# Attention's weighing in 32 bits, the experts' second bias on VectorE, and a combination with four neighbouring tokens per partition

## What is computed

```python
q, k, v = (qkv[0] * scale, qkv[1], qkv[2])        # 16 heads of 8 channels
# logits over the 7 x 7 neighbours of a pixel, plus a relative bias
attn = softmax(logits, -1)
out = sum_t attn[..., t, None] * v_at_neighbour_t
x = x + (out @ proj_w.T + proj_b)
probs = softmax(layernorm(x) @ W_router); topk_p, topk_i = top_k(probs, 2)
for e in range(8):
    h = relu(x_flat @ W1[e] + b1[e])               # 128 -> 512
    y = h @ W2[e] + b2[e]                          # 512 -> 128
    out = out + combine[:, e:e + 1] * y
```

## Time and profile before

| | |
|---|---|
| median of 3 runs | 3155.05 us (3146.11 to 3156.77) |
| the profiled execution | 3149.2 us, its span 3147.4 us |
| mean granted TensorE clock | 0.904 |
| busy: PE, DVE, ACT, POOL | 79%, 75%, 67%, 75% of the span |
| attention | from the start to about 2300 us |
| experts | about 2366 to 2963 us |
| combination | about 2963 us to the end |

### The profile page before, as it was taken

The page is one execution under the profiler, slowest core; times in us unless marked ns, Lnnn a source line. Parts: engine busy times, 40 slices in busy tenths (PEclk is TensorE's granted clock), DMA queues, the critical chain, the costliest instruction groups (busy, mean ns, idle before and its releaser), DMA issues. The chain is left out here.

```text
span 3147.4 us, 119476 instructions
## 1 busy us (share of the span) xinstructions
PE 2482.8 (79%) x34587; PEld 2108.7 (67%) x34692; DVE 2353.8 (75%) x12579; ACT 2122.5 (67%) x5724; POOL 2360.1 (75%) x2808
## 2 busy tenths in 40 slices
PE   4788887888788878888888878888709999999633
PEld 2677777777777777777777777777606666666522
DVE  2688887888788878888788878888746666666444
ACT  0677777777677777777777777777726777777400
POOL 2578888888888888888888888888946777777600
PEclk9999999999899999999999989999959999999855
DMA  2566555555555655555565555556455444444499
GB/s 49 145 126 119 121 124 119 114 122 118 112 106 122 123 118 110 118 117 117 114 120 118 118 109 119 121 117 123 92 99 94 93 92 93 93 93 92 98 314 299
DMA packets 743654, 378.47 MB, mean 120 GB/s; under 512 B 414595, under 2 KB 712227, under 8 KB 743078
## 3 DMA queue, kind: packets, MB, share of 16 engines
q1 hardware_dynamic: 690278, 235.46, 39.5%
q10 hardware_dynamic: 24192, 81.67, 9.9%
q0 software_dynamic: 28608, 54.48, 5.7%
HBM read 232.92 MB, written 98.11 MB: 105 GB/s over the span
## 5 line engine op out<-in xcount | busy, mean ns | idle before, releaser
L1004 ACT ACTIVATE pr<-sc,nmx 128x100 f32<-128x100 f32 x3136 | 922.3, 369 | 103.8 <-DVE nmx L670 100.6
L905 POOL TENSOR_TENSOR pl<-pt 100x512 f16<-100x512 f32 x784 | 815.3, 1040 | 217.9 <-ACT pt L1012 217.4
L670 DVE CUSTOM_DVE_ANT_0 sc<-bank,near 128x100 f32<-128x100 f32 x3136 | 632.3, 256 | 182.7 <-PE bank L490 133.4
L1012 ACT ACTIVATE pt<-bank 100x512 f32<-100x512 f32 x784 | 462.5, 590 | 365.9 <-PE bank L516 353.0
L490 PE MATMUL bank<-kimg,qexp 128*128 (+2 forms) x9408 | 651.5, 221 | 55.3 <-issue 40.0
L490 PEld LDWEIGHTS bank<-kimg,qexp 128*128 128x128 bf16 (+1 forms) x9408 | 567.7, 102 | 103.1 <-issue 71.7
L1385 POOL DMA_INDIRECT yrows<-ye,meta x420 | 451.1, 1074 | 188.6 <-issue 127.6
L516 PE MATMUL bank<-vwin,pt 100*128 100x65 bf16 (+1 forms) x6272 | 417.0, 199 | 202.7 <-DVE om L700 142.6
L516 PEld LDWEIGHTS bank<-vwin,pt 100*128 100x128 bf16 x6272 | 371.9, 102 | 277.1 <-issue 184.6
L911 POOL TENSOR_TENSOR oml<-om 128x256 f16<-128x256 f32 x784 | 483.4, 617 | 57.3 <-DVE om L700 35.4
L499 PE MATMUL bank<-cst_sb,pr 128*100 128x128 f32 x3136 | 503.9, 286 | 0.0
(11 more groups left out here) (150 smaller groups left out, 4665.4 us busy)
## 6 DMA issues: line engine op xcount, KB each, us to landing
vwin<-v_pix SPq DMA_DIRECT2D x1120, 60.5 KB
near<-bias_rows ACTq DMA_DIRECT2D x112, 600.0 KB
y<-yrows SPq DMA_DIRECT2D x112, 224.0 KB, 4.8
qexp<-qring SPq DMA_DIRECT2D x896, 14.0 KB
v_pix<-vrow SPq DMA_DIRECT2D x56, 225.8 KB
xin<-in_x SPq DMA_DIRECT2D x56, 224.0 KB
xres<-in_x SPq DMA_DIRECT2D x112, 112.0 KB, 4.6
x<-xres SPq DMA_DIRECT2D x112, 112.0 KB
```

The lines of the kernel that those rows point to most:

```text
L670: i = v.tensor_tensor_reduce(out=sc[:, ring(m, par), k, :], in0=ps_s[m % 2][:, k, :], in1=near[:, st, ct, k, :], scale=-1.0, scalar=-MASKE ...
L905: g.tensor_tensor(pl[:, m % 2], pt[:, m % 2], pt_h[:, m % 2], ALU.subtract).then_inc(s["t_out"], 1)
L1004: i = a.activation(pr[:, r, k, :], sc[:, r, k, :], ACT.Exp, bias=nmx[:, r, k:k + 1], scale=-1.0)
L1012: i = a.activation(pt[:, m % 2].rearrange("p a q -> p (a q)"), ps_t[m % 2][0:NKEY, :], ACT.Copy)
```

## The change

Three edits. In attention, `v_pix`, `vrow` and `vwin` hold 32-bit numbers (129 a pixel); `weigh` multiplies `pt` and `vwin` as they are, one 32-bit product for each block; `split_t`, `a_v_l` and the buffer `pl` are gone, and every station behind the transposes stands one step earlier. In the experts, the product for the second bias is gone and DVE adds the bias in PSUM, from a table `b2b` with all experts' biases on every partition, before it multiplies. In the combination, a partition holds four neighbouring tokens, so its rows of `y` are 2048 bytes in one piece, and DVE's last sum reorders the columns; the first four loads of x1 are issued before SP waits for the last scatters.

```diff
-L_T, L_V, L_P, L_H, L_F = 3, 5, 6, 7, 8
+L_T, L_V, L_P, L_H, L_F = 3, 4, 5, 6, 7
-        v_pix = nc.dram_tensor("v_pix", (B * IMG, 2, VW), BF16, kind="Internal").ap()
+        v_pix = nc.dram_tensor("v_pix", (B * IMG, VW), FP32, kind="Internal").ap()
-        vwin = asb("vwin", [NKEY, 2, NTILE, 2, VW], BF16)
+        vwin = asb("vwin", [NKEY, 2, NTILE, VW])
-        vrow = asb("vrow", [HALF, NROW, 2, VW], BF16)
+        vrow = asb("vrow", [HALF, NROW, VW])
-        pl = asb("pl", [NKEY, 2, 4, 128], FP16)
...
                 def weigh(J, m, par):
-                    pe.wait_ge(s["t_out"], n + 1)
+                    pe.wait_ge(s["th_done"], n + 1)
...
-                            p_h, p_l = pt_h[:, m % 2, 2 * t + blk, :], pl[:, m % 2, 2 * t + blk, :]
-                            v_h, v_l = (vwin[:, st, 2 * u + t, part, 64 * blk:64 * blk + 65].bitcast(dt)
-                                        for part, dt in enumerate((BF16, FP16)))
-                            for n, (a_, b_) in enumerate(((p_h, v_h), (p_h, v_l), (p_l, v_h))):
-                                mm = pe.matmul(ps_av[m % 2][:, 2 * t + blk, :], a_, b_, start=n == 0, stop=n == 2)
+                            mm = pe.matmul(ps_av[m % 2][:, 2 * t + blk, :], pt[:, m % 2, 2 * t + blk, :],
+                                           vwin[:, st, 2 * u + t, 64 * blk:64 * blk + 65], start=True, stop=True)
...
-                def a_v_l(I):
...
-                LATE_STEPS = {9: a_q_l, 10: a_k_l, 12: a_v_l}
+                LATE_STEPS = {9: a_q_l, 10: a_k_l}
...
-                def split_t(J, m, par):
-
-                    n = UPP * J + m
-                    g.wait_ge(s["th_done"], n + 1)
-                    g.tensor_tensor(pl[:, m % 2], pt[:, m % 2], pt_h[:, m % 2], ALU.subtract).then_inc(s["t_out"], 1)
...
-                        i = a.activation(vrow[:, :, 0, 65 * blk:65 * blk + 64],
+                        i = a.activation(vrow[:, :, 65 * blk:65 * blk + 64],
...
-                    i.then_inc(s["v_h"], 1)
+                    i.then_inc(s["v_out"], 1)
...
-                sp.wait_ge(s["b2_step"], 1)
-                for k in range(3):
-                    sp.dma_start(b2f[32 * k:32 * k + 1, :], b2).then_inc(s["b2_in"], 16)
+                sp.dma_start(b2b[:], bass.AP(b2.tensor, 0, [[0, 128], [1, E * C]])).then_inc(s["b2_in"], 16)
...
+                for r in range(ZR):
+                    sp.dma_start(xo[:, r, :], x1[:, r * TOK:(r + 1) * TOK]).then_inc(s[f"z_x{r}"], 16)
                 for r in range(XR):
                     sp.wait_ge(s[f"m_sc{r}"], 16 * 4 * ((NT - r + XR - 1) // XR))
...
-                        src = bass.AP(yrows.tensor, c * (TOK * C) + j * (NTOK * C), [[C, HALF], [HALF * C, QT], [1, C]])
-                        sp.dma_start(dst[:, r], src).then_inc(s[f"z_x{r}"], 16)
-                    sp.dma_start(xo[:, r, :], x1[:, bass.ds(c * TOK, TOK)]).then_inc(s[f"z_x{r}"], 16)
+                        src = bass.AP(yrows.tensor, c * (TOK * C) + j * (NTOK * C), [[QT * C, HALF], [1, QT * C]])
+                        sp.dma_start(dst[:, r].rearrange("p n c -> p (n c)"), src).then_inc(s[f"z_x{r}"], 16)
+                    if not early(c, ZR):
+                        sp.dma_start(xo[:, r, :], x1[:, bass.ds(c * TOK, TOK)]).then_inc(s[f"z_x{r}"], 16)
...
-                    pe.matmul(o[:, :], three[:], b2s[:, bass.ds(e * C, C)].unsqueeze(1).to_broadcast([128, 4, C]),
-                              start=True, stop=False)
...
-                def gated(i, r):
+                def gated(i, r, e):
                     v.wait_ge(s["m_y"], i + 1)
+                    y = ps_y[r % 2].rearrange("p (g c) -> p g c", c=C)
+                    v.tensor_tensor(y, y, b2b[:, bass.ds(e * C, C)].unsqueeze(1).to_broadcast([128, 4, C]), ALU.add)\
+                        .then_inc(s["m_yb"], 1)
...
+                    v.wait_ge(s["m_yb"], i + 1)
...
+                        before = v.value_load(e_tab[0:1, bass.ds(i - 1, 1)], min_val=0, max_val=E - 1)
+                        gated(i - 1, (r - 1) % MR, before)
...
-                    v.tensor_tensor(oo[:, par], bank[6 + par][:, 0:TOK], xo[:, r], ALU.add).then_inc(s["z_out"], 1)
+                    v.tensor_tensor(oo[:, par].rearrange("c (p n) -> c n p", n=QT),
+                                    bank[6 + par][:, 0:TOK].rearrange("c (n p) -> c n p", n=QT),
+                                    xo[:, r].rearrange("c (p n) -> c n p", n=QT), ALU.add).then_inc(s["z_out"], 1)
```

More of the change, by code:

```diff
@@ L218, in build @@
         names = """w_in w_scaled w1_in cst_in rpb_in pad_out gath_in turned win_in bias_done zeroed pad_zero
-            x_in mean_done xc_done sq_done v_h sub_done th_done oml_done
+            x_in mean_done xc_done sq_done sub_done th_done oml_done
             var_done ve_done root_done spread_done xn_done q_done q_h q_out k_done k_h k_out v_done v_out v_store q_exp0 q_exp1
-            v_in0 v_in1 s_done max_done exp_done t_done t_out av_done rec_done orec_done om_done
+            v_in0 v_in1 s_done max_done exp_done t_done av_done rec_done orec_done om_done
             o_done o_out proj_done proj_out bias_out near_in0 near_in1 xres_in0 xres_in1 x1_store0 x1_store1
@@ L312, in store_v @@
                     sp.wait_ge(s["v_out"], I + 1)
-                    dst = bass.AP(v_pix.tensor, I * (PAIR * 2 * VW), [[2 * VW, HALF], [HALF * 2 * VW, NROW], [1, 2 * VW]])
-                    sp.dma_start(dst, vrow[:].rearrange("p n a c -> p n (a c)")).then_inc(s["v_store"], 16)
+                    dst = bass.AP(v_pix.tensor, I * (PAIR * VW), [[VW, HALF], [HALF * VW, NROW], [1, VW]])
+                    sp.dma_start(dst, vrow[:]).then_inc(s["v_store"], 16)
                 def spread_q(J, par):
@@ L332, in windows @@
                         sp.wait_ge(s["av_done"], UPP * J - UPP + UNITS * (st + 1))
[L333 removed]
+                    at = ((J // NPAIR) * IMG + krow(J, st) * W) * VW
                     for kr in range(KW):
[L335 to L336 removed]
+                        src = bass.AP(v_pix.tensor, at + (kr * W + 1) * VW, [[VW, KW], [TS * VW, NTILE - 2], [1, VW]])
+                        sp.dma_start(vwin[kr * KW:(kr + 1) * KW, st, 1:NTILE - 1], src).then_inc(s[f"v_in{st}"], 16)
                     for t, c0 in ((0, 0), (NTILE - 1, W - KW)):
[L338 to L339 removed]
+                        src = bass.AP(v_pix.tensor, at + c0 * VW, [[W * VW, KW], [VW, KW], [1, VW]])
+                        sp.dma_start(vwin[:, st, t], src).then_inc(s[f"v_in{st}"], 16)
                 def load_res(J, st):
@@ L604, in _ @@
                 v.memset(qexp[:, 1].rearrange("p s t h q -> p (s t h q)"), 0.0).then_inc(s["zeroed"], 1)
-                v.memset(vrow[:, :, 1, 64:65], 0.0)
-                v.memset(vrow[:, :, 0, 64:65], 1.0).then_inc(s["pad_zero"], 1)
+                v.memset(vrow[:, :, 64:65], 1.0).then_inc(s["pad_zero"], 1)
                 v.memset(ones_b[:], 1.0)
@@ L917, in body @@
                                 subtract(J, m, par)
-                            for d, step in ((L_H, split_l), (L_T, split_t)):
-                                if reached(J, m, d):
-                                    step(*back(J, m, par, d))
+                            if reached(J, m, L_H):
+                                split_l(*back(J, m, par, L_H))
                         if I is not None and m == A_ROOT:
@@ L931, in _ @@
                 for m in range(L_H):
-                    for d, step in ((L_H, split_l), (L_T, split_t)):
-                        if m < d:
-                            step(*back(PAIRS, m, PAIRS % 2, d))
+                    split_l(*back(PAIRS, m, PAIRS % 2, L_H))
                 for Q in range(PAIRS - 3, PAIRS):
@@ L1106, in build @@
         stage2 = sb("stage2", [128, E * FF])
[L1107 to L1111, removed]
+        b2b = sb("b2b", [128, E * C])
         b1_sb = sb("b1_sb", [128, E * FC])
@@ L1248, in second @@
                             for n, (a_, b_) in enumerate(((hh, w2h), (hh, w2l), (hl, w2h))):
-                                mm = pe.matmul(o[:, g * C:(g + 1) * C], a_[:, slot, tok], b_[:, w], start=False,
+                                mm = pe.matmul(o[:, g * C:(g + 1) * C], a_[:, slot, tok], b_[:, w], start=f == 0 and g == 0 and n == 0,
                                                stop=f == FC - 1 and g == 3 and n == 2)
@@ L1274, in _ @@
             def _(v):
-                v.memset(b2f[:], 0.0).then_inc(s["b2_step"], 1)
-                v.memset(three[:], 0.0)
-                v.memset(b2s[:], 0.0)
-                v.drain()
-                for k in range(3):
-                    v.memset(three[32 * k:32 * k + 1, :], 1.0)
                 def tables():
@@ L1312, in splits @@
                     v.tensor_tensor(w2l[:], stage2[:], w2h[:], ALU.subtract).then_inc(s["split2"], 1)
-                    v.wait_ge(s["b2_in"], 48)
-                    v.tensor_copy(b2p[:, 0], b2f[:])
-                    v.drain()
-                    v.tensor_tensor(b2r[:], b2f[:], b2p[:, 0], ALU.subtract)
```

(16 more changed lines are left out.)

6 lines of the change are left out of this document (2 added, 4 removed).

## The result

The changed kernel takes **3047.45 us** (median of four runs, 3044.93 to 3050.45) where the kernel before took 3155.91 beside it (four runs): ratio 0.966, 95% interval 0.963 to 0.969, 108 us less. Its profiled execution took 3044.93 us with a span of 3043.1. The forecast was 3074, the range 3000 to 3165.

The account below looks back on a forecast made before the run. It took PE to bound the experts, and several engines waiting for each other attention. Attention -38, experts -22, combination -19, between stages +2 gave -77 from 3149.2, 3072, plus 2 for the runs' median: 3074 us, range 3000 to 3165.

Parts of the forecast that it names:

- the hole behind step 11: Attention: PE idles after DVE's long step 11 and its clock falls; expected to close, saving 3.2 us a pair.
- rival 1: Attention: PE's clock still falls, a pair takes 41.8 us, total about 3235 us; chance 0.14.
- Rival 2: Attention: the shorter lag stalls PE in steps 9 to 13, 1.0 to 1.7 us a pair more, 3123 to 3157; chance 0.17.
- I take 0.92: Attention: weigh's four 32-bit products take 0.92 us a unit, between 0.89 and 0.96, so +7.8 us a pair.
- 0.7 us a pair where the loop turns: Attention: PE's wait for issue at the loop's turn costs 0.7 us a pair, and that stays.
- 37.5 + 0.7 + 0.3 = 38.5: Attention, us a pair: PE's work with the new weigh, the loop's turn, and waits for ACT; 0.9 below 39.4.
- POOL issues every 1.27 us: Experts: POOL's scatters take 0.97 + 0.30 us each, 5.08 us a tile, below the new 5.47.
- POOL's scatter starts later but not slower: Experts: with the bias added by DVE, POOL's scatter only starts later; part of the 22 us saving.
- the early loads: Combination: four loads moved ahead of the wait for the last scatters, 0.9 MB, save 3 us.
- 59 against 47 ns per KB: Combination: y's longer rows lower SP's queue price to that of ACT's queue; 16 us taken of the stage's -19.
- Rival 3: Combination: rows of four tokens bring nothing, the stage gives 3 us, total 3090; chance 0.14.
- The same operation in another order of addresses: Combination: DVE's sum with reordered columns stays the same operation, beside the transfers; no cost was added.

Follow-up runs that it names:

- idle_pool_load: The changed kernel plus, for each unit, a GpSimd subtraction of split_t's size into a buffer nobody reads: 3490.46 us, ratio 1.1087.
- x1_once: The changed kernel with the combination loading x1 for its first four chunks alone, later chunks reusing those blocks: 3033.92 us (one run).
- four_oo_pe_order: The changed kernel with four output buffers in the combination and the column order put right in PE's transposes, not VectorE's last sum: 3049.48 us.

## Why the prediction was right, and where its steps were not

**The mechanism of attention held.** What the forecast named came: PE becomes the fullest engine (96%), ACT's wait for `weigh` goes, `gapr` falls to 0.15 us, the hole behind step 11 closes and the clock rises to 0.98. Away from the turns it is 1.00, with the 32-bit products. idle_pool_load shows the other side: with POOL's load put back, rival 1 happens, hole and clock as described, and dearer than its 3235 us. Rival 2 did not come: PE waits 18 us in 1200 for `om`, its loader 25 for `pt`.

**The price of `weigh` was too high.** The step "I take 0.92" measured 0.84, below both ends (0.89 and 0.96). I had scaled L438 by its columns and then leaned to L448, which moves 112 columns; at 0.105 a record `weigh` lies under L438 scaled to 128 columns (0.111), so its 65 columns add nothing that shows. 0.08 us in 784 units is 63 us. The Trainium skill, "TensorE: Matmul & The Clock Gate", section on LDWEIGHTS, gives 107 ns for 128 columns; the trace has 105, so here the page was nearer than my rows.

**The loop was priced too low.** "0.7 us a pair where the loop turns" counted the wait alone. The turn also costs the clock behind it: over the five turns the two pairs at one take 83.1 us on average, against 74.3 for two others, so 8.9 us a turn, 0.9 a pair over all 49. And I had no term at all for working inside the loop, 1.05 us a pair. A pair then comes out as 36.05 + 1.05 + 0.9 = 38.0, as measured (1863.2 / 49), where I had 37.5 + 0.7 + 0.3 = 38.5. So the two misses partly cancelled. Of the edges the last pairs gained more than I gave them, and the first three lost less; the first pair's 44.2 us is 54.1 in x1_once with the same attention, so part of that is chance.

**The experts** gave 18.4 of the 22, the mechanism as forecast: DVE's cover sufficed and PE is busy 98%. Tiles are 5.53 us apart, for the 5.4 to 5.5 expected. "POOL issues every 1.27 us", 5.08 a tile, was read from one row and is too low: over the stage a scatter keeps POOL busy for 1.08 us on average, with 0.30 behind it, so 5.5 us a tile, as long as the tile itself. In the changed kernel POOL has no rest left there. Its waits in 500 us of the stage, the changed kernel's first and then the one before's:

```profile
POOL yrows L1347 <- issue: 91.2, 299, 0.3
...
POOL yrows L1347 <- DVE ye L1302: 19.2, 63, 0.3
```

```profile
POOL yrows L1385 <- issue: 108.1, 339, 2.0
```

None of the 362 waits is longer than the 0.3 us between two issues; before, the longest was 2.0. PE does not wait for it, but at the end "POOL's scatter starts later but not slower" was wrong. The last instructions of POOL and VectorE there:

```profile
2868.01 0.69 DVE L1302 TENSOR_TENSOR ye<-bank,meta 128x512 f32<-128x512 f32 x1
```

```profile
2877.27 0.97 POOL L1347 DMA_INDIRECT yrows<-ye,meta  x1 [0.31 <-issue]
2878.54 0.97 POOL L1347 DMA_INDIRECT yrows<-ye,meta  x1 [0.30 <-issue]
2879.82 0.97 POOL L1347 DMA_INDIRECT yrows<-ye,meta  x1 [0.30 <-issue]
```

POOL issues its last scatter 12.8 us behind PE's last product at 2867.0 (8.4 before), for it had two whole tiles and more in hand. The combination waits for those scatters, so the early loads did not show.

**The combination was the step that failed most**, -5.7 for -19. I priced `y`'s rows by the time that packets take in a queue, 59 against 47 ns per KB. That price did fall (82.1% of 16 x 130 us on 31.92 MB is 54), and the chunks hardly followed (2.75 us at 327 GB/s, for the 2.6 at above 340 expected). The two queues' shares add to 109.8% in the earlier trace rows and to 104.8% now: packets of both are under way at once, so their time is no time of the engines that adds up to the stage. Rival 3 was the better account; by runs, rows of four tokens bring 0.06 us a chunk with four buffers and some 0.1 with two (2.87, 2.95 and 2.91 us in three profiles against 2.75 to 2.87 in seven). The Trainium skill, "DMA: Bandwidth & Descriptors", Specifications, has line rate from 512 bytes; the runs agree to within some 4%. "The same operation in another order of addresses" was wrong for VectorE's last sum (0.96 us for 0.62), but with four buffers four_oo_pe_order shows that it cost no time.

In sum the time came 27 us below the forecast: attention 43 lower, the experts and the combination 17 higher, the rest between the stages 1 lower. That the result lies within 3040 to 3105 is in part luck: with the later stages as forecast it would have been 3030.

## What to carry to other kernels

An engine's load can cost more than its queue: before moving work to or from GpSimd, look for small VectorE instructions that take microseconds beside it, and for PE's granted clock behind the hole that they make. Price a 32-bit product with few moving columns by its weight loads, and a transfer by the rate of its stage, not by packet time in one queue. When PE is the bound, the loop around it is the next thing to price: here one pass gave 95 us, nearly as much as the whole change.

## What the runs showed of the hardware

- A product of four numbers a partition on VectorE takes 0.15 us in the changed kernel and 3.10 us beside a run of GpSimd subtractions, longer than any one of them (1.04 us). The Trainium skill, "SBUF — State Buffer", Who interferes with whom, says that a VectorE instruction with two SBUF inputs contends with a GpSimd instruction that reads SBUF, over a shared pair of ports that works as an exclusive lock. The rows agree with the contention and go beyond the sentence: the small one of the earlier trace rows ended with GpSimd's second subtraction, so it waited through several of the others.
- PE idle for 3.9 us at a loop's turn is followed by some 10 us at a granted clock of 0.50; a turn costs 8.9 us on average, about half of it behind the wait.
- Four 32-bit products with 128 stationary and 65 moving columns take 0.84 us in eight records; with 16-bit halves alone a pair is only 3 us shorter.
- Inside a hardware loop a pair took 37.1 us, with the same work in one pass 36.05.
- A sum of 128x448 numbers on VectorE takes 0.96 us with columns in another order and 0.62 us in plain order.
